# Row statistics of the first phase: joining and centring moved from VectorE to GpSimd, eight tiles at once, with longer leads

## The chip, the cores and the metric

One NeuronCore of one Trainium2 chip runs the whole program. The metric is the device time of one execution in microseconds (us). Three executions of the kernel before took 3013.57, 3014.26 and 3014.30 us.

## The reference

An adaptive-LayerNorm transformer block in fp32: x is 16 x 1024 x 256 (16 batches of 1024 rows).

```python
sa, ca, ga, sb, cb, gb = modulations of each batch            # from silu(c) @ wmod
h = layernorm(x) * (1 + ca) + sa                              # first statistics: of the rows of x
def attention(h):                                             # causal, 16 heads of 16, with rope
    hn = (h - mean(h)) * rsqrt(var(h) + 1e-5) * gamma + beta  # second statistics: of the rows of h
    q, k, v = hn @ Wq + bq, hn @ Wk + bk, hn @ Wv + bv        # rope on q and k
    return h + softmax(mask(q k^T / 4)) v @ Wo + bo
x = x + ga * attention(h)
x = x + gb * mixture_of_experts(layernorm(x) * (1 + cb) + sb) # 8 experts, 512 rows each, first two batches' rows
```

So each row of 256 values is normalised twice before the projections: once as x, once as h.

## The kernel before

The program is a chain of phases with a barrier between them: phase 0 (weights, tables, modulations), phase 1 (both normalisations, projections to q, k and v, rope, stores), phase 2 (attention), phase 3 (output projection and second residual), phase 4 (experts). The diff touches phase 1 alone, which lies between about 58 and 562 us of the span.

Phase 1 takes the 16 batches one after the other. A batch is 8 tiles of 128 rows x 256 columns (T = 8) and 4 pairs (NP = 4: q and k of each half of 512 rows). The work is laid out by hand in slots, 8 to a batch: each engine runs `slot(s)` for s from START to END in order, and each step is put into a slot by its lead: `batch_at(s, lead)` gives the batch b and the place k with s + lead = 8b + k, so a step of lead 17 comes 17 slots ahead of the slot in which projections of its batch begin. Nothing holds the engines to the same slot but semaphores; within an engine the order is fixed, and a step that waits holds up all behind it.

One batch passes through these steps (leads of the kernel before in brackets):

- SyncE `load`: x of the batch, 1 MB, into a ring of three buffers `xin`, and its modulation rows. A load waits until GpSimd has read the batch three earlier. The order in SyncE's queue is: loads 0 to 3, then for each b load b+4, the stores of b.
- VectorE `take_x` (23): `bn_stats` of two tiles in each of four slots. It gives for each row the mean of the even and of the odd columns and their sums of squared deviations (6 numbers).
- VectorE `join_x` (in take_x's last slot, L458): eight `bn_aggr`, one per tile, to mean and variance.
- ScalarE `root` (19, L554): sqrt(var + eps) of 8 tiles at once. VectorE `invert_x` (18): reciprocal (L463) and the centring term -mean/std (L465), each for 8 tiles at once.
- ScalarE `first_norm` (17, L559), one tile per slot; GpSimd `modulate` (16): times 1 + ca (L635), plus sa (L638). For batch 0 the addition is VectorE's (L473).
- VectorE `take_h` (15, L477): `bn_stats` of one tile of h per slot; `join_h` (with the last of them, L482); `root` (7); `invert_h` (6, L488, L490); ScalarE `second_norm` from lead 5 on (L566).
- TensorE transposes the tiles (L662), projects q and k (`project`, even slots, L673) and v (`values`, odd slots, L681); ScalarE copies the transposed tiles and v out of PSUM (L574, L583).
- VectorE `multiply` (odd slots, L501 and L504, four instructions of 512 columns) and `combine` (even slots, L511, L512) do the rope in PSUM. Then a split of q and k into three bf16 parts: ScalarE `high` (L591), VectorE `take_rest` (L517), ScalarE `middle` (L595), GpSimd `low` (L642, 1024 columns, even slots).
- SyncE stores v (4 DMAs), the q parts (8) and the k parts (8) of the batch.

Buffers that tie engines together: `rest` has two halves (take_rest of pair n waits for low of pair n-2), PSUM holds three pairs, `stage` and `v_st` hold two batches.

Of the kernel before, what the change touches and what calls it, by code (L numbers as in the profile page):

```python
# [17 lines left out]
F32 = mybir.dt.float32  # L18
# [3 lines left out]
ALU = mybir.AluOpType  # L22
ACT = mybir.ActivationFunctionType
# [303 lines left out]
def phase1(nc, x, ps, ident, cos_t, sin_t, w_all, bcol, rsx, nmx, mods_d, q_d, k_d, v_d):  # L327
# [11 lines left out]
    with ExitStack() as ctx:  # L339
# [5 lines left out]
        h = sb("h", [P, 2, T, D], F32)  # L345
        stx = sb("stx", [P, T, 6], F32)
        sth = sb("sth", [P, T, 6], F32)
        agx = sb("agx", [P, 2, T, 2], F32)
        agh = sb("agh", [P, 2, T, 2], F32)
        rsh = sb("rsh", [P, 2, T], F32)  # L350
        nmh = sb("nmh", [P, 2, T], F32)
        sd = sb("sd", [P, 2, T], F32)
# [8 lines left out]
        mod_in = tuple(sem(f"p1_mod_in{r}") for r in range(RING))  # L361
        stx_done, sth_done = sem("p1_stx"), sem("p1_sth")
        agx_done, agh_done = sem("p1_agx"), sem("p1_agh")
        sdx_done, sdh_done = sem("p1_sdx"), sem("p1_sdh")
        rsx_done, rsh_done = sem("p1_rsx"), sem("p1_rsh")
        ones_set = sem("p1_ones_set")
# [20 lines left out]
        def turned(n):  # L387
            return ps[:, PS_QK + n % QR * 2:PS_QK + n % QR * 2 + 2, :]

        START = -23  # L390
        END = B * T + 6

        def batch_at(s, lead):

            b, k = (s + lead) // T, (s + lead) % T
            return (b, k) if 0 <= b < B else (None, None)
# [10 lines left out]
        @block.sync  # L407
        def _(sp):
            def load(b):
                r = b % RING  # L410
                if b == RING:
                    sp.wait_ge(first_done, T)
                elif b > RING:
                    sp.wait_ge(h_done, (b - RING) * T)
                sp.dma_start(xin[:, r], x[b].rearrange("(t p) d -> p t d", p=P)).then_inc(x_in[r], DMA)
                sp.dma_start(mods[:, r], mods_d[b, 0:2, :].partition_broadcast(P)) \
                  .then_inc(mod_in[r], DMA)

            def store(b):
                p = b % 2  # L420
                sp.wait_ge(v_copied, b * T + T)
                for g in range(NG):
                    sp.dma_start(v_d[b, g], v_st[:, p, g].rearrange("p t n -> p (t n)")).then_inc(v_stored[p], DMA)
                for which, dst in enumerate((q_d, k_d)):
                    last = b * NP + NP - 2 + which
                    sp.wait_ge(hi_done, last + 1)
                    sp.wait_ge(mid_done, last + 1)
                    sp.wait_ge(lo_done, last + 1)
                    for e in range(2):
                        for g in range(NG):  # L430
                            sp.dma_start(dst[b, g, :, 32 * e:32 * e + 32, :].rearrange("s r t -> r s t"),
                                         stage[32 * g:32 * g + 32, p, :, 2 * which + e, :]).then_inc(stage_stored[p], DMA)

            for b in range(RING + 1):
                load(b)
            for b in range(B):
                if b + RING + 1 < B:
                    load(b + RING + 1)
                store(b)
            for p in range(2):  # L440
                sp.wait_ge(v_stored[p], DMA * NG * (B // 2))
                sp.wait_ge(stage_stored[p], DMA * STORES * (B // 2))

        @block.vector
        def _(dve):
# [6 lines left out]
                    ins = dve.bn_stats(stx[:, t, :], xin[:, r, t, :])  # L452
                ins.then_inc(stx_done, 1)

            def join_x(b):
                dve.wait_ge(stx_done, 4 * b + 4)
                for t in range(T):
                    ins = dve.bn_aggr(agx[:, b % 2, t, :], stx[:, t, :])  # L458
                ins.then_inc(agx_done, 1)

            def invert_x(b):
                dve.wait_ge(sdx_done, b + 1)
                dve.reciprocal(rsx[:, b, :], sd[:, 0, :]).then_inc(rsx_done, 1)  # L463
                dve.wait_ge(rsx_done, b + 1)
                dve.scalar_tensor_tensor(nmx[:, b, :], agx[:, b % 2, :, 0], -1.0, rsx[:, b, :], ALU.mult, ALU.mult) \  # L465
                   .then_inc(statx, 1)

            def take_h(b, t):
                if t == 0:
# [6 lines left out]
                    dve.wait_ge(h_done, (b - 1) * T + t + 1)  # L476
                dve.bn_stats(sth[:, t, :], h[:, b % 2, t, :]).then_inc(sth_done, 1)  # L477

            def join_h(b):
                dve.wait_ge(sth_done, b * T + T)  # L480
                for t in range(T):
                    ins = dve.bn_aggr(agh[:, b % 2, t, :], sth[:, t, :])  # L482
                ins.then_inc(agh_done, 1)

            def invert_h(b):
                p = b % 2
                dve.wait_ge(sdh_done, b + 1)
                dve.reciprocal(rsh[:, p, :], sd[:, 1, :]).then_inc(rsh_done, 1)  # L488
                dve.wait_ge(rsh_done, b + 1)
                dve.scalar_tensor_tensor(nmh[:, p, :], agh[:, p, :, 0], -1.0, rsh[:, p, :], ALU.mult, ALU.mult) \  # L490
                   .then_inc(stath, 1)

            def multiply(n):

# [24 lines left out]
            def slot(s):  # L519
                n = (s - 1) // 2  # L520
                if s % 2 == 1 and 0 <= n < B * NP:
                    multiply(n)
                n = (s - 2) // 2
                if s % 2 == 0 and 0 <= n - 1 < B * NP:
                    take_rest(n - 1)
                if s % 2 == 0 and 0 <= n < B * NP:
                    combine(n)
                b, k = batch_at(s, 18)
                if b is not None and k == 0:
                    invert_x(b)  # L530
                b, k = batch_at(s, 6)
                if b is not None and k == 0:
                    invert_h(b)
                b, k = batch_at(s, 15)
                if b is not None:
                    take_h(b, k)
                    if k == T - 1:
                        join_h(b)
                b, k = batch_at(s, 23)
                if b is not None and k < 4:  # L540
                    take_x(b, k)
                    if k == 3:
                        join_x(b)

            dve.memset(eps[:, :], EPS)
            for s in range(START, END):
# [1 line left out]

        @block.scalar
        def _(act):  # L550
            def root(b, which, ag, ready, done):
                reuse(act, rsh_done if which else rsx_done, b)
                act.wait_ge(ready, b + 1)
                nc.scalar.activation(sd[:, which, :], ag[:, b % 2, :, 1], ACT.Sqrt, bias=eps[:, :]).then_inc(done, 1)  # L554

            def first_norm(b, t):
                if t == 0:
# [37 lines left out]
                nc.scalar.copy(parts(n, 1), rest[:, n % 2]).then_inc(mid_done, 1)  # L595

            def slot(s):
                b, k = batch_at(s, 19)
                if b is not None and k == 0:
                    root(b, 0, agx, agx_done, sdx_done)  # L600
                b, k = batch_at(s, 7)
                if b is not None and k == 0:
                    root(b, 1, agh, agh_done, sdh_done)
                for tiles, b in turned_in(s - 1):
                    for t in tiles:
                        copy_x(b, t, tiles[-1])
                n = (s - 3) // 2
                if s % 2 == 1 and 0 <= n < B * NP:
                    high(n)
                if s % 2 == 0 and 2 <= s <= B * T:  # L610
                    for t in (s - 2, s - 1):
                        copy_v(t // T, t % T)
                n = (s - 5) // 2
                if s % 2 == 1 and 0 <= n < B * NP:
                    middle(n)
                b, k = batch_at(s, 17)
                if b is not None:
                    first_norm(b, k)
                for tiles, b in normed_in(s):
                    for t in tiles:  # L620
                        second_norm(b, t)
# [5 lines left out]
        @block.gpsimd  # L627
        def _(pool):
            def modulate(b, t):
                p, r = b % 2, b % RING  # L630
                if t == 0:
                    pool.wait_ge(mod_in[r], (b // RING + 1) * DMA)
                reuse(pool, xt_done, (b - 2) * T + t + 1)
                pool.wait_ge(h1_done, b * T + t + 1)
                pool.tensor_tensor(h[:, p, t, :], xin[:, r, t, :], mods[:, r, M_CA1, :], ALU.mult).then_inc(h_mul, 1)  # L635
                if b > 0:
                    pool.wait_ge(h_mul, b * T + t + 1)
                    pool.tensor_tensor(h[:, p, t, :], h[:, p, t, :], mods[:, r, M_SA, :], ALU.add).then_inc(h_done, 1)  # L638

            def low(n):  # L640
                pool.wait_ge(mid_done, n + 1)
                pool.tensor_tensor(parts(n, 2), rest[:, n % 2], parts(n, 1), ALU.subtract).then_inc(lo_done, 1)  # L642

            def slot(s):
                b, k = batch_at(s, 16)
                if b is not None:
                    modulate(b, k)
                n = (s - 6) // 2
                if s % 2 == 0 and 0 <= n < B * NP:
                    low(n)  # L650

            pool.memset(v_st[:, :, :, :, :], 1.0).then_inc(ones_set, 1)
            for s in range(START, END + 1):
                slot(s)
# [1031 lines left out]
```

## Time and profile before

| | |
|---|---|
| median of 3 runs | 3014.26 us (3013.57 to 3014.30) |
| profiled execution, its own time | 3013.66 us |
| its span | 3011.9 us |
| TensorE busy over the span | 2753.8 us, 91% |
| VectorE | 2140.9 us, 71% |
| ScalarE | 1825.3 us, 61% |
| GpSimd | 974.6 us, 32% |

The span is that of the recorded instructions; the execution's own time is 1.76 us longer. Shares of the whole span say little about one phase. In phase 1, from 100 to 500 us, VectorE is busy more than 98.7 us of each 100, TensorE 83 to 86, ScalarE 68 to 72, GpSimd 65 to 69. "Busy" is the time of an instruction; engines start the next instruction a little before the recorded end of the last, so the step from start to start is often 0.04 to 0.09 us shorter than the duration.

### The profile page before, as it was taken

The numbers are of one execution on the slowest core, as the hardware profiler recorded it, in microseconds if no ns is written. First come the engines' busy times: TensorE is split into PE (matmuls) and PEld (weight loads), VectorE is DVE, ScalarE is ACT, GpSimd is POOL, SyncE is SP. The second block draws the span as 40 slices with busy tenths as digits, with TensorE's granted clock in tenths as the row PEclk, the third lists the DMA queues.
The fourth block names the chain that finished last, engine by engine and source line by source line (L and its number), as shares of the span: only waits on it lengthen the run. The fifth ranks groups of instructions, "written<-read, shape, count | busy, mean of one in ns | idle before, by whom it ended". The sixth has DMA issues, their size and how long they took to land. (4 is left out here: it accounts for less than half of the span.)

```text
span 3011.9 us, 48208 instructions
## 1 busy us (share of the span) xinstructions
PE 2753.8 (91%) x17467; PEld 1341.3 (45%) x17467; DVE 2140.9 (71%) x3145; ACT 1825.3 (61%) x3739; POOL 974.6 (32%) x1298
## 2 busy tenths in 40 slices
PE   1788889499999999999999999999999879998997
PEld 0454445234444444444444444444444346775664
DVE  4999999587777777777777777777777436652221
ACT  1676677157777777777777777777777744441121
POOL 1666666312212212212212212212211247771331
PEclk7899999689999999999999999999999989999999
DMA  3367676824454354454454455354345068962342
GB/s 97 119 221 231 220 233 210 214 50 93 87 108 93 88 106 94 87 106 94 88 105 95 89 104 99 86 103 98 88 102 102 25 227 291 312 224 58 99 109 44
DMA packets 186485, 384.09 MB, mean 128 GB/s; under 512 B 33397, under 2 KB 102421, under 8 KB 173736
## 3 DMA queue, kind: packets, MB, share of 16 engines
q1 hardware_dynamic: 180106, 372.48, 48.2%
q0 software_dynamic: 6144, 8.52, 1.6%
q8 instruction: 141, 2.31, 0.3%
q14 instruction: 94, 0.77, 0.1%
HBM read 238.55 MB, written 144.53 MB: 127 GB/s over the span
## 5 line engine op out<-in xcount | busy, mean ns | idle before, releaser
L929 DVE TENSOR_REDUCE mx<-ps 128x2 f32<-128x1024 f32 (+3 forms) x1216 | 1371.5, 1167 | 396.9 <-PE ps L1017 301.7
L975 ACT ACTIVATE prob<-ps 128x512 f32<-128x512 f32 (+1 forms) x2560 | 1251.8, 560 | 538.8 <-PE ps L1035 530.1
L1010 PE MATMUL ps<-k_rows,q_rows 96*128 96x512 bf16 (+3 forms) x3072 | 911.2, 332 | 41.0 <-DMA k_rows<-k_parts 34.4
L1035 PE MATMUL ps<-q_rows,k_rows 99*128 99x512 bf16 (+3 forms) x3072 | 907.2, 328 | 14.7 <-ACT prob L975 6.1
L868 POOL TENSOR_SCALAR_AFFINE_SELECT prob<-prob 128x512 f32<-128x512 f32 x512 | 320.0, 637 | 1451.3 <-ACT prob L975 1451.3
L1054 PE MATMUL ps<-prob,v_rows 128*32 128x512 f32 (+3 forms) x6144 | 628.3, 496 | 0.0
L1035 PEld LDWEIGHTS ps<-q_rows,k_rows 99*128 99x128 bf16 x3072 | 273.1, 98 | 599.0 <-ACT prob L975 360.3
L1010 PEld LDWEIGHTS ps<-k_rows,q_rows 96*128 96x128 bf16 x3072 | 290.2, 98 | 271.4 <-DVE mx L929 60.5
L1017 PE MATMUL ps<-mask_b,unit_b 128*128 128x128 bf16 (+2 forms) x1408 | 348.6, 248 | 0.0
L673 PE MATMUL ps<-x_t,w_all 128*128 128x512 f32 x512 | 249.8, 634 | 0.0
L1054 PEld LDWEIGHTS ps<-prob,v_rows 128*32 128x32 f32 x6144 | 134.3, 108 | 245.8 <-ACT prob L975 122.9
L1548 DVE SCALAR_TENSOR_TENSOR y<-ps,gx,gate 128x256 f32<-128x256 f32 x32 | 15.5, 484 | 196.4 <-PE ps L1637 196.4
L1017 PEld LDWEIGHTS ps<-mask_b,unit_b 128*128 128x128 bf16 x1408 | 139.5, 99 | 22.9
L673 PEld LDWEIGHTS ps<-x_t,w_all 128*128 128x128 f32 x512 | 101.8, 207 | 105.0 <-issue 104.1
L642 POOL TENSOR_TENSOR stage<-rest,stage 128x1024 bf16<-128x1024 f32 x64 | 136.5, 2133 | 30.1 <-ACT stage L595 30.1
L1398 PE MATMUL ps<-wg,n_t 128*128 128x256 f32 x512 | 145.7, 407 | 0.0
L662 PE MATMUL ps<-ident,h 128*128 128x128 f32 x256 | 49.7, 302 | 102.3 <-ACT x_t L574 64.6
L1332 ACT COPY n_t<-ps 128x256 f32<-128x256 f32 x128 | 47.5, 371 | 148.6 <-PE ps L1386 148.3
L635 POOL TENSOR_TENSOR h<-xin,mods_b 128x256 f32<-128x256 f32 x128 | 94.0, 736 | 133.0 <-ACT xin L559 133.0
L681 PE MATMUL ps<-w_all,x_t 128*128 128x256 f32 x512 | 121.2, 379 | 0.0
L1473 POOL DMA_INDIRECT sum_rows<-ys,dest x32 | 50.4, 1574 | 212.8 <-ACT ys L1560 156.0
L1637 PE MATMUL ps<-w,hid 128*128 128x256 f32 x512 | 119.1, 386 | 0.0
(154 smaller groups left out, 2678.1 us busy)
## 6 DMA issues: line engine op xcount, KB each, us to landing
k_rows<-k_parts SPq DMA_DIRECT2D x384, 128.0 KB, 7.3
v_ones<-v_st SPq DMA_DIRECT2D x64, 512.0 KB, 4.3
v_rows<-v_ones SPq DMA_DIRECT2D x64, 512.0 KB, 9.1
att<-o_sb SPq DMA_DIRECT2D x128, 256.0 KB, 2.4
att_b<-att SPq DMA_DIRECT2D x16, 2048.0 KB, 10.1
q_parts<-stage SPq DMA_DIRECT2D x128, 192.0 KB, 3.3
k_parts<-stage SPq DMA_DIRECT2D x128, 192.0 KB, 3.3
q_rows<-q_parts SPq DMA_DIRECT2D x64, 384.0 KB, 4.6
```

Source lines behind the costliest of these rows:

```text
L642: pool.tensor_tensor(parts(n, 2), rest[:, n % 2], parts(n, 1), ALU.subtract).then_inc(lo_done, 1)
L673: ins = pe.matmul(half(n, e), w_all[:, k, c * P:(c + 1) * P], x_t[:, blk, k, :], start=(k == 0), stop=(k == KC - 1))
L681: ins = pe.matmul(o, x_t[:, t // 4, k, t % 4 * P:t % 4 * P + P], w_all[:, k, 2 * D:3 * D], start=(k == 0), stop=(k == KC - 1))
L868: pool.affine_select(out=own, in_=own, compare_op=ALU.is_ge, fill=0.0, base=0, pattern=[[0, HG], [1, P]], channel_multiplier=-1).then_inc( ...
L929: dve.tensor_reduce(dst, src, AX.X, ALU.max).then_inc(a_free, 1)
L975: nc.scalar.activation(prob[:, (g * NPC + i) % RING, h, 0:w], src, ACT.Exp).then_inc(exp_done, 1)
L1010: ins = pe.matmul(ps[:, at, col:col + w], q[0:ROWS, g, h, i * P:(i + 1) * P], k[0:ROWS, g, h, k0:k0 + w], start=(r == 0), stop=True, skip_ ...
L1017: ins = pe.matmul(own, unit_b[:, :], mask_b[:, :].rearrange("p (o n) -> p o n", o=1) .to_broadcast([P, per, P]), start=False, stop=True, s ...
L1035: ins = pe.matmul(ps[:, PS_B + bank(g, n), at:at + w], k[0:AUG, g, h, j * P:(j + 1) * P], q[0:AUG, g, h, q0:q0 + w], start=True, stop=True)
L1054: ins = pe.matmul(ps[32 * h:32 * h + 32, PS_O, col:col + w], v[:, g, j, h, :], prob[:, (g * NPC + i) % RING, h, at:at + w], start=(j == 0) ...
L1398: ins = pe.matmul(o, n_t[:, r % 2, k, :], wg[:, p, k, :], start=False, stop=(k == KC - 1))
L1637: ins = pe.matmul(o, hid[:, f, c * P:(c + 1) * P], w2[:, e % 2, f, :], start=False, stop=(f == FT - 1))
```

## The change

- The eight `bn_aggr` of a batch, for x and for h, go. GpSimd computes the same from the two half-row means and sums of squares with seven instructions over 128 x 8 values (`join`): sums, difference and spread; then the squared difference times D/4 is added to the spread; and -0.5 times the sum of means is kept as `half_sum`. Four of the seven are followed by a wait on their own semaphore (`link`). The result is 256 times the variance, and `root` scales by 1/256.
- The centring term -mean/std becomes a GpSimd product `half_sum` * reciprocal (`centre`) in a slot of its own, instead of VectorE's scalar_tensor_tensor. The reciprocals stay on VectorE.
- Leads grow: take_x 23 to 27, its join now at 23, root 22, invert 21, centre 20; first_norm 17 to 19, modulate 16 to 18, take_h 15 to 17; join of h at 9, root 8, invert 7, centre 6. second_norm and everything behind it keep theirs. START goes from -23 to -27.
- SyncE has the loads of batches 0 to 4 ahead of the first store, and load b+5 ahead of the stores of b.

```diff
-            def join_x(b):
-                dve.wait_ge(stx_done, 4 * b + 4)
-                for t in range(T):
-                    ins = dve.bn_aggr(agx[:, b % 2, t, :], stx[:, t, :])
-                ins.then_inc(agx_done, 1)
             def invert_x(b):
                 dve.wait_ge(sdx_done, b + 1)
                 dve.reciprocal(rsx[:, b, :], sd[:, 0, :]).then_inc(rsx_done, 1)
-                dve.wait_ge(rsx_done, b + 1)
-                dve.scalar_tensor_tensor(nmx[:, b, :], agx[:, b % 2, :, 0], -1.0, rsx[:, b, :], ALU.mult, ALU.mult) \
-                   .then_inc(statx, 1)
...
             def invert_h(b):
-                p = b % 2
                 dve.wait_ge(sdh_done, b + 1)
-                dve.reciprocal(rsh[:, p, :], sd[:, 1, :]).then_inc(rsh_done, 1)
-                dve.wait_ge(rsh_done, b + 1)
-                dve.scalar_tensor_tensor(nmh[:, p, :], agh[:, p, :, 0], -1.0, rsh[:, p, :], ALU.mult, ALU.mult) \
-                   .then_inc(stath, 1)
+                reuse(dve, xn_done, (b - 1) * T)
+                dve.reciprocal(rsh[:, b % 2, :], sd[:, 1, :]).then_inc(rsh_done, 1)
...
-            for b in range(RING + 1):
+            for b in range(RING + 2):
                 load(b)
             for b in range(B):
-                if b + RING + 1 < B:
-                    load(b + RING + 1)
+                if b + RING + 2 < B:
+                    load(b + RING + 2)
                 store(b)
...
+            def link(ins):
+                links[0] += 1
+                ins.then_inc(pool_chain, 1)
+                pool.wait_ge(pool_chain, links[0])
+
+            def join(b, which, st, ready, count, rooted, done):
+                pool.wait_ge(ready, count)
+                reuse(pool, rooted, b)
+                pool.tensor_tensor(sums[:, which, :], st[:, :, 1], st[:, :, 4], ALU.add)
+                pool.tensor_tensor(gap[:, which, :], st[:, :, 1], st[:, :, 4], ALU.subtract)
+                link(pool.tensor_tensor(spread[:, which, :], st[:, :, 2], st[:, :, 5], ALU.add))
+                link(pool.tensor_scalar(half_sum[:, which, :], gap[:, which, :], D / 4.0, None, ALU.mult))
+                link(pool.tensor_tensor(gap[:, which, :], gap[:, which, :], half_sum[:, which, :], ALU.mult))
+                link(pool.tensor_scalar(half_sum[:, which, :], sums[:, which, :], -0.5, None, ALU.mult))
+                pool.tensor_tensor(spread[:, which, :], spread[:, which, :], gap[:, which, :], ALU.add).then_inc(done, 1)
+
+            def centre(which, nm, rs):
+                return pool.tensor_tensor(nm, half_sum[:, which, :], rs, ALU.mult)
...
             def slot(s):                       # GpSimd
-                b, k = batch_at(s, 16)
+                b, k = batch_at(s, 23)
+                if b is not None and k == 0:
+                    join(b, 0, stx, stx_done, 4 * b + 4, sdx_done, agx_done)
+                b, k = batch_at(s, 9)
+                if b is not None and k == 0:
+                    join(b, 1, sth, sth_done, b * T + T, sdh_done, agh_done)
+                b, k = batch_at(s, 20)
+                if b is not None and k == 0:
+                    pool.wait_ge(rsx_done, b + 1)
+                    centre(0, nmx[:, b, :], rsx[:, b, :]).then_inc(statx, 1)
+                b, k = batch_at(s, 6)
+                if b is not None and k == 0:
+                    pool.wait_ge(rsh_done, b + 1)
+                    reuse(pool, xn_done, (b - 1) * T)
+                    centre(1, nmh[:, b % 2, :], rsh[:, b % 2, :]).then_inc(stath, 1)
+                b, k = batch_at(s, 18)
                 if b is not None:
                     modulate(b, k)
```

## Rows read from the trace of the kernel before

**Rows 1.** Busy time in two batch-long stretches; columns: length, then engines, clock, DMA.
```profile
141.10:170.30 29.20, 22.78 (x80) 13.47 (x80) 29.06 (x68) 20.48 (x42) 19.81 (x20) 1.00 0.72 226
287.30:316.50 29.20, 25.63 (x80) 14.77 (x80) 28.34 (x57) 20.60 (x42) 19.80 (x20) 0.88 0.69 219
```
**Rows 2.** Waits from 98 to 506 us: total us, times, longest.
```profile
POOL h L635 <- ACT xin L559: 122.5, 43, 6.0
...
DVE m L501 <- PE ps L673: 4.1, 3, 3.2
```
**Rows 3.** Instruction groups from 98.62 to 506 us: count, busy us, mean ns, idle before.
```profile
L465 DVE SCALAR_TENSOR_TENSOR nmx<-agx,rsx 128x8 f32<-128x8 f32 x13 | 21.7, 1671 | 0.4
L490 DVE SCALAR_TENSOR_TENSOR nmh<-agh,rsh 128x8 f32<-128x8 f32 x14 | 10.6, 758 | 0.5
L482 DVE BATCH_NORM_AGGREGATE agh<-sth 128x2 f32<-128x6 f32 x112 | 9.0, 153 | 0.5
L458 DVE BATCH_NORM_AGGREGATE agx<-stx 128x2 f32<-128x6 f32 x104 | 8.3, 153 | 0.4
```
**Rows 4.** VectorE in order of time: start, duration, instruction, count.
```profile
307.56 0.20 DVE L488 RECIPROCAL rsh<-sd 128x8 f32<-128x8 f32 x1
307.79 0.75 DVE L490 SCALAR_TENSOR_TENSOR nmh<-agh,rsh 128x8 f32<-128x8 f32 x1
308.46 0.41 DVE L477 BATCH_NORM_STATS2 sth<-h 128x6 f32<-128x256 f32 x1
...
315.72 0.73 DVE L452 BATCH_NORM_STATS2 stx<-xin 128x6 f32<-128x256 f32 x2
316.48 0.64 DVE L458 BATCH_NORM_AGGREGATE agx<-stx 128x2 f32<-128x6 f32 x8
317.04 1.38 DVE L501 SCALAR_TENSOR_TENSOR m<-ps,bcol,cos_t 128x512 f32<-128x512 f32 x2
```
**Rows 5.** All instructions of L465: shortest, median and longest duration.
```profile
L465 DVE SCALAR_TENSOR_TENSOR nmx<-agx,rsx x16: 166/1670/1677, 69.8 to 468.3; 128x8 f32<-128x8 f32 x16
```
**Rows 6.** GpSimd in order of time, within one batch.
```profile
322.05 2.13 POOL L642 TENSOR_TENSOR stage<-rest,stage 128x1024 bf16<-128x1024 f32 x1
324.14 0.73 POOL L635 TENSOR_TENSOR h<-xin,mods_b 128x256 f32<-128x256 f32 x1
324.95 0.73 POOL L638 TENSOR_TENSOR h<-h,mods_b 128x256 f32<-128x256 f32 x1
325.63 0.73 POOL L635 TENSOR_TENSOR h<-xin,mods_b 128x256 f32<-128x256 f32 x1
```
**Rows 7.** GpSimd's smallest instructions: two of phase 2, one at the start.
```profile
606.96 0.28 POOL L876 CAST m<-m_rest 32x128 bf16<-32x128 f32 x1 [30.27 <-DVE m_rest L912]
607.32 0.42 POOL L878 TENSOR_TENSOR m<-m_rest,m 32x128 bf16<-32x128 f32 x1
...
L1674 POOL MEMSET const-float32-0.0<- 128x1 f32 x1 | 0.1, 104 | 0.3 <-issue 0.3
```
**Rows 8.** TensorE in order of time: projection, four transposes (two tiles), values.
```profile
308.15 3.60 PE L673 MATMUL ps<-x_t,w_all 128*128 128x512 f32 x8
311.59 0.60 PE L662 MATMUL ps<-ident,h 128*128 128x128 f32 x4
312.02 1.89 PE L681 MATMUL ps<-w_all,x_t 128*128 128x256 f32 x8
```
**Rows 9.** Start of phase 1: GpSimd's first multiplications of h; VectorE's first rope instructions.
```profile
70.76 4.50 POOL L635 TENSOR_TENSOR h<-xin,mods_b 128x256 f32<-128x256 f32 x6 [5.32 <-ACT xin L559]
...
98.62 1.41 DVE L501 SCALAR_TENSOR_TENSOR m<-ps,bcol,cos_t 128x512 f32<-128x512 f32 x2 [3.21 <-PE ps L673]
```
**Rows 10.** One load of x: issue, first use; loads from 100 to 500 us, to landing.
```profile
319.79 0.69 SPq L415 DMA_DIRECT2D xin<-in_L_attn_x  x1
...
333.69 0.41 DVE L452 BATCH_NORM_STATS2 stx<-xin 128x6 f32<-128x256 f32 x1
...
xin<-in_L_attn_x SPq DMA_DIRECT2D x11, 1024.0 KB, 7.7
```

More of the change, by code:

```diff
@@ L347, in phase1 @@
         sth = sb("sth", [P, T, 6], F32)
-        agx = sb("agx", [P, 2, T, 2], F32)
-        agh = sb("agh", [P, 2, T, 2], F32)
+        sums = sb("sums", [P, 2, T], F32)
+        gap = sb("gap", [P, 2, T], F32)
+        spread = sb("spread", [P, 2, T], F32)
+        half_sum = sb("half_sum", [P, 2, T], F32)
         rsh = sb("rsh", [P, 2, T], F32)
@@ L363, in phase1 @@
         agx_done, agh_done = sem("p1_agx"), sem("p1_agh")
+        pool_chain = sem("p1_pool_chain")
         sdx_done, sdh_done = sem("p1_sdx"), sem("p1_sdh")
@@ L388, in turned @@
             return ps[:, PS_QK + n % QR * 2:PS_QK + n % QR * 2 + 2, :]
-        START = -23
+        START = -27
         END = B * T + 6
@@ L477, in take_h @@
                 dve.bn_stats(sth[:, t, :], h[:, b % 2, t, :]).then_inc(sth_done, 1)
[L479 to L483, printed above, removed]
             def invert_h(b):
-                p = b % 2
                 dve.wait_ge(sdh_done, b + 1)
-                dve.reciprocal(rsh[:, p, :], sd[:, 1, :]).then_inc(rsh_done, 1)
-                dve.wait_ge(rsh_done, b + 1)
-                dve.scalar_tensor_tensor(nmh[:, p, :], agh[:, p, :, 0], -1.0, rsh[:, p, :], ALU.mult, ALU.mult) \
-                   .then_inc(stath, 1)
+                reuse(dve, xn_done, (b - 1) * T)
+                dve.reciprocal(rsh[:, b % 2, :], sd[:, 1, :]).then_inc(rsh_done, 1)
             def multiply(n):
@@ L527, in slot @@
                     combine(n)
-                b, k = batch_at(s, 18)
+                b, k = batch_at(s, 21)
                 if b is not None and k == 0:
                     invert_x(b)
-                b, k = batch_at(s, 6)
+                b, k = batch_at(s, 7)
                 if b is not None and k == 0:
                     invert_h(b)
-                b, k = batch_at(s, 15)
+                b, k = batch_at(s, 17)
                 if b is not None:
                     take_h(b, k)
-                    if k == T - 1:
-                        join_h(b)
-                b, k = batch_at(s, 23)
+                b, k = batch_at(s, 27)
                 if b is not None and k < 4:
                     take_x(b, k)
-                    if k == 3:
-                        join_x(b)
             dve.memset(eps[:, :], EPS)
@@ L550, in _, with root @@
         def _(act):
-            def root(b, which, ag, ready, done):
+            def root(b, which, ready, done):
                 reuse(act, rsh_done if which else rsx_done, b)
                 act.wait_ge(ready, b + 1)
-                nc.scalar.activation(sd[:, which, :], ag[:, b % 2, :, 1], ACT.Sqrt, bias=eps[:, :]).then_inc(done, 1)
+                nc.scalar.activation(sd[:, which, :], spread[:, which, :], ACT.Sqrt, bias=eps[:, :], scale=1.0 / D).then_inc(done, 1)
             def first_norm(b, t):
@@ L597, in slot @@
             def slot(s):
-                b, k = batch_at(s, 19)
+                b, k = batch_at(s, 22)
                 if b is not None and k == 0:
-                    root(b, 0, agx, agx_done, sdx_done)
-                b, k = batch_at(s, 7)
+                    root(b, 0, agx_done, sdx_done)
+                b, k = batch_at(s, 8)
                 if b is not None and k == 0:
-                    root(b, 1, agh, agh_done, sdh_done)
+                    root(b, 1, agh_done, sdh_done)
                 for tiles, b in turned_in(s - 1):
@@ L615, in slot @@
                     middle(n)
-                b, k = batch_at(s, 17)
+                b, k = batch_at(s, 19)
                 if b is not None:
@@ L638, in modulate @@
                     pool.tensor_tensor(h[:, p, t, :], h[:, p, t, :], mods[:, r, M_SA, :], ALU.add).then_inc(h_done, 1)
+            links = [0]
+            def link(ins):
[14 more added lines that the diff above has]
+                return pool.tensor_tensor(nm, half_sum[:, which, :], rs, ALU.mult)
             def low(n):
```

## The prediction

> **What bounds the kernel now.** The page shows TensorE busy 91% of the span and VectorE 71%, but the diff touches only phase 1, so I read that phase alone. The busy time by batch-long windows comes first: in a batch of 29.2 us VectorE is busy 29.06, TensorE 22.78 where its clock was full, ScalarE 20.5, GpSimd 19.8 [rows 1]. The waits say the same from the other side: from the first rope instruction to 506 us VectorE waited 4.1 us in all, 3.2 of them ahead of the first, while GpSimd waited 122.5 us for ScalarE, which follows VectorE [rows 2]. So phase 1 goes at VectorE's pace, and an instruction taken from VectorE there is worth its own step. Nothing later in the program depends on when phase 1 ends except by starting then, so what phase 1 gains the program gains.
>
> **What the change removes from VectorE.** A step is start to start; the end of a recorded duration lies about 0.08 us behind the next start (0.75 from 307.79 ends at 308.54, the next starts at 308.46 [rows 4]).
> - Joins: eight bn_aggr. The statistics ahead of them start at 315.72 and would hand over after 0.73 - 0.08 = 0.65, at 316.37; the next real work starts at 317.04: 0.67, call it 0.66. After the first rope there are 104/8 = 13 joins of x and 112/8 = 14 of h [rows 3]: 8.6 + 9.2 = 17.8 us.
> - Centring term of h: reciprocal and product take 307.56 to 308.46 = 0.90 [rows 4]; the reciprocal alone, which stays, 0.20 - 0.08 = 0.12. So 0.78 each, with the mean of the product in the group near that of this one (758 ns): 14 x 0.78 = 11.0 us.
> - Centring term of x: the mean duration is 1671 ns, against 166 ns for the same instruction at its shortest [rows 3, 5]. It stretches while GpSimd works at a `low` of 2.13 us: its two inputs are both in SBUF. Its step with the gap ahead is 1.67 + 0.04 = 1.71; 13 x 1.71 = 22.2 us. Nothing on VectorE in steady state has two SBUF inputs after the change (rope and rest read one of theirs from PSUM), so that stretch does not come back elsewhere.
> Sum: 51.0 us, and VectorE's batch becomes 29.2 - 2 x 0.66 - 0.78 - 1.71 = 25.4 us.
>
> **What it adds to GpSimd.** No row shows an elementwise GpSimd instruction on 128 x 8. Bounds from the nearest: 0.10 (memset of one column) and 0.42 (subtraction of 32 x 128) [rows 7]. From L635 and L642, 0.73 at 256 columns and 2.13 at 1024 [rows 6], a straight line leaves 0.26 at none; from 0.42 at 128 and 0.73 at 256 it leaves 0.11. I take 0.20, between them. A wait for its own semaphore adds 0.08 (606.96 + 0.28 = 607.24, next at 607.32); without one the next starts 0.04 early (324.95 + 0.73 against 325.63). A join is then 2 x 0.16 + 4 x 0.28 + 0.20 = 1.64 us (bounds 1.0 and 3.2), a centring product 0.20 (0.1 to 0.42).
> GpSimd's batch now: a tile is 0.81 + 0.68 = 1.49, a `low` 2.09 [rows 6]: 8 x 1.49 + 4 x 2.09 = 20.3. New: 20.3 + 2 x 1.64 + 2 x 0.20 = 24.0 us (22.5 to 27.5), under VectorE's 25.4, but only by 1.4. Its free time was 9 us a batch; that is what hides the joins, and if each cost 2.4 it would be used up (20.3 + 4.8 + 0.4 = 25.5).
>
> **What queues behind the new waits.** In slot 1 of a batch GpSimd waits for the last statistics of x, done at the end of VectorE's slot 0. So the two are in step there once a batch. Walking GpSimd from that point (VectorE's 25.4 us spread over its slots by what each holds: 2.7 and 3.1 by turns, 3.6 and 3.3 where two tiles of x, 0.65, are added): its slots end at 3.1, 6.9, 8.4, 12.2, 13.7, 17.3, then join of h to 19.5 (it starts with VectorE's last bn_stats of h, 17.8), 21.0, 24.6. Next comes the wait to 25.4. Each tile of h is needed by VectorE late in the slot after, each `low` at the start of two slots after (slot 2's at 8.9, done 6.9): all in time. ScalarE has 20.5 us of work in 25.4 and now finds the joins a slot early; it does not stick. The reciprocal gets new waits that are a batch old: nothing.
> The Trainium skill speaks against this move: "Perfetto Trace Analysis", section "Optimizing Scalar/DVE Operations", says that work moved between VectorE and GpSimd may not help, since both share a read port. Here the row of the stretched product agrees that they block each other, but the change takes away the only VectorE instruction that was blocked; by that rule the products' 33 us would come back as GpSimd waits, and the gain would be near 15 us. Nothing above or below uses this.
>
> **TensorE** needs for a batch four projections of 3.44, four `values` of 1.73 (1.89 less the same overlap), and eight tiles at 0.215 [rows 8]: 22.4 us at full clock; in a batch of granted clock 0.88 that would be 25.4, a tie [rows 1].
>
> **Loads.** A load was issued at 319.79, needed at 333.69, and lands in 7.7: 6.2 us to spare [rows 10]. New: load c stands behind the k stores of batch c-6, whose last `low` is in slot 8c-36, with take_x in 8c-27, that is 8 slots or 25.4 us later. Less some 6 us of store issues and 7.7, 11 us to spare. The edit costs nothing. DMA share rises from 0.72 to 0.72 x 29.2/25.4 = 0.83, still not full.
>
> **The start.** Leads grow, so more precedes the first rope. First tile of h on GpSimd: was 70.76 [rows 9]; the chain before it loses 0.67 and 0.2, gains 1.64, 0.20 and a hop: 71.96. From there GpSimd runs to the second tile of batch 2, which VectorE needs in slot 0: 8 multiplications at 0.75 (4.50/6), then 10 tiles at 1.49, four joins, three products, and about 2.3 us of waits for statistics: 6.0 + 14.9 + 6.6 + 0.6 + 2.3 = 30.4, at 102.4. VectorE then has a bn_stats of h and a pair of x (0.34 + 0.65): first rope at 103.4, against 98.62: 4.8 later. In exchange VectorE has done 2 bn_stats of h and 4 pairs of x more by then: 0.7 + 2.6 = 3.3 us not to be done later.
>
> **The end.** From 506 us on nothing of the statistics is left and VectorE's work on a pair is under TensorE's 5.2 (3.44 + 1.73); the statistics of x end four slots earlier and of h two, so VectorE meets TensorE's pace sooner: I put 1.5 us on it, four such slots at some 0.4. Closing stores and barrier are unchanged. For new small waits in steady state, 2 us.
>
> **Sum** against the profiled execution: 3013.66 - 51.0 - 3.3 + 4.8 + 1.5 + 2 = 2967.7; against the median 3014.26 (0.6 above) 2968.3. I say 2968.
>
> **Rivals.**
> A. GpSimd becomes the bound. For: only 1.4 us of slack and no row of such a size. Against: the straight lines put an instruction at 0.11 to 0.26. With every price at its upper row a join is 3.2, a product 0.42, the batch 27.5: 13 x 1.7 = 22 gained, less 1.5 at the start and 4 x 1.6 more there: 14 us gained, 3000. At a join of 2.6 the batch is 26.0, the gain 13 x 3.2 - 1.5 - 4 - 2 = 34, 2980.
> B. TensorE becomes the bound, by its clock. For: granted clock 0.88 in one batch; against: that batch held a long idle of TensorE, which goes with ScalarE's sticking. At 0.85 a batch is 26.3: 0.9 x 13 = 12 us less, 2980.
> C. Slower: the chain of sixteen GpSimd instructions a batch, at y us each with waits, holds up the tiles of h. The gain is 13 x (29.2 - 20.3 - 16y), less 1.5 and 4 x (7y - 1.64) at the start; it is nil at y = 0.51. At y = 0.60 a batch is 29.9, and the time 13 x 0.7 + 1.5 + 10.2 = 21 us more, 3035. For: nothing but the upper row with its wait, 0.50. Against: the same lines.
> D. VectorE's time turns into waits in a loop over GpSimd and ScalarE, which show no more than today's pace: 3012.
>
> **Chances.** Forecast (2959 to 2975) 0.62, A 0.18, B 0.12, C 0.04, D 0.04. The low end is joins at 1.0 (start 2.6 sooner) and no small waits or tie: 2962, less 3 for the sizes of steps. The high end, 2996, takes in B and most of A. Faster by over 0.2% (6 us, about what a measurement of this kernel can tell) 0.92, within it 0.04, slower 0.04.
>
> **What would show it.** Batches of 25.4 us in phase 1, with VectorE busy about 25 of them; joins of about 1.6 us on GpSimd and GpSimd busy 23 to 24; first L501 near 103.4; phase 2 starting 46 us earlier. A VectorE that waits for GpSimd's h at every tile means A; waits at L501 for TensorE mean B. The prediction is wrong if the batch stays above 26 us.

## The result and the profile after

The changed kernel takes 2964.84 us (2964.05 to 2966.78, four runs) against 3014.28 us for the kernel before beside it: ratio 0.9835, 95% interval 0.9823 to 0.9847, that is 49 us less. The forecast was 2968, with 2959 to 2996. The profiled execution took 2965.41 us, its span is 2963.7 (before: 3013.66 and 3011.9), so the two traces differ by 48.2 us. One of the executions of the half-statistics kernel below ran at a granted clock of 0.83 and took 3243.83 us against 2947 to 2952 for the other three, and is not in its median.

First, two batch-long stretches of phase 1 in the changed kernel, to hold against [rows 1] (same columns):

```profile
core 0: us, PE busy (x) PEld busy (x) DVE busy (x) ACT busy (x) POOL busy (x), PEclk, DMA share, GB/s
260.94:286.13 25.19, 24.02 (x80) 13.38 (x80) 25.19 (x47) 20.30 (x43) 22.84 (x37) 1.00 0.85 257
286.13:311.32 25.19, 24.01 (x80) 13.40 (x80) 25.19 (x47) 20.30 (x43) 22.84 (x37) 1.00 0.88 271
```

The batch is 25.19 us, and VectorE is busy for all of it. ScalarE's work is what it was; GpSimd's busy time went from 19.8 to 22.8. TensorE is busy 24.0 us, at full clock. The waits from 103 to 460 us, the answer to [rows 2]:

```profile
ACT stage L572 <- DVE ps L497: 62.2, 41, 1.8
...
PE ps L680 <- ACT x_t L555: 9.4, 11, 0.9
...
POOL sums L632 <- DVE stx L455: 8.6, 12, 0.8
...
POOL sums L632 <- DVE sth L471: 3.7, 12, 1.6
...
DVE sth L471 <- POOL spread L638: 2.1, 1, 2.1
DVE m L486 <- PE ps L691: 1.6, 2, 1.0
```

VectorE itself stands 4.1 us in the whole window; the others wait for it, directly or through ScalarE. GpSimd, which stood 122.5 us for ScalarE, now waits where it needs VectorE's last statistics, once a batch 0.7 us for those of x and 0.3 us for those of h. In the kernel before, ScalarE stood at the head of its slot in `root` for VectorE's joins, up to 4.1 us at a time, and TensorE for ScalarE's copies of the transposed tiles, up to 4.3 us (98 to 506 us):

```profile
ACT sd L554 <- DVE agx L458: 51.4, 13, 4.1
PE ps L662 <- ACT x_t L574: 61.3, 24, 4.3
```

The second became 9.4 us with 0.9 at the longest; the first is gone from the steady batches.

VectorE's order of time around the reciprocals, for [rows 4], where joins and products are gone:

```profile
284.82 1.45 DVE L489 SCALAR_TENSOR_TENSOR ps<-ps,bcol,sin_t 128x512 f32<-128x512 f32 x2
286.13 0.23 DVE L476 RECIPROCAL rsh<-sd 128x8 f32<-128x8 f32 x1
286.24 0.42 DVE L471 BATCH_NORM_STATS2 sth<-h 128x6 f32<-128x256 f32 x1
286.54 1.25 DVE L502 TENSOR_TENSOR rest<-ps,stage 128x1024 f32<-128x1024 f32 x1
...
291.81 0.23 DVE L460 RECIPROCAL rsx<-sd 128x8 f32<-128x8 f32 x1
291.92 0.42 DVE L471 BATCH_NORM_STATS2 sth<-h 128x6 f32<-128x256 f32 x1
```

GpSimd's join of x and what follows it, the instructions for which [rows 7] gave only bounds:

```profile
283.71 0.21 POOL L632 TENSOR_TENSOR sums<-stx 128x8 f32<-128x8 f32 x1 [0.75 <-DVE stx L455]
283.88 0.21 POOL L633 TENSOR_TENSOR gap<-stx 128x8 f32<-128x8 f32 x1
284.05 0.21 POOL L634 TENSOR_TENSOR spread<-stx 128x8 f32<-128x8 f32 x1
284.34 0.23 POOL L635 TENSOR_SCALAR half_sum<-gap 128x8 f32<-128x8 f32 x1
284.66 0.20 POOL L636 TENSOR_TENSOR gap<-gap,half_sum 128x8 f32<-128x8 f32 x1
284.95 0.23 POOL L637 TENSOR_SCALAR half_sum<-sums 128x8 f32<-128x8 f32 x1
285.26 0.20 POOL L638 TENSOR_TENSOR spread<-spread,gap 128x8 f32<-128x8 f32 x1
285.42 0.72 POOL L616 TENSOR_TENSOR h<-xin,mods_b 128x256 f32<-128x256 f32 x1
286.22 0.73 POOL L619 TENSOR_TENSOR h<-h,mods_b 128x256 f32<-128x256 f32 x1
286.91 0.20 POOL L641 TENSOR_TENSOR nmh<-half_sum,rsh 128x8 f32<-128x8 f32 x1
```

An instruction takes 0.20 to 0.23 us, a step is 0.17 without a wait and 0.29 to 0.32 with one, the join 283.71 to 285.42 = 1.71 us.

Last the start, from the changed kernel's VectorE and GpSimd, for [rows 9]:

```profile
60.15 0.06 DVE L526 MEMSET eps<- 128x1 f32 x1 [2.01 <-PEq L122]
...
103.97 0.43 DVE L471 BATCH_NORM_STATS2 sth<-h 128x6 f32<-128x256 f32 x1 [2.12 <-POOL spread L638]
...
107.23 1.41 DVE L486 SCALAR_TENSOR_TENSOR m<-ps,bcol,cos_t 128x512 f32<-128x512 f32 x2 [0.69 <-PE ps L691]
```
```profile
73.79 2.27 POOL L616 TENSOR_TENSOR h<-xin,mods_b 128x256 f32<-128x256 f32 x3 [0.78 <-ACT xin L540]
78.11 0.31 POOL L632 TENSOR_TENSOR sums<-stx 128x8 f32<-128x8 f32 x1 [2.05 <-DVE stx L455]
```

The 48.2 us by part, from the two traces. Phase 1 begins for VectorE (the memset of eps) at 58.58 before and 60.15 after, 1.57 later; the same code ran ahead of it, the twelve runs below put it between 58.07 and 59.59, and a second run of the unaltered changed kernel is one of them, at 58.56, so this is no part of the change. From there to the first rope 40.04 became 47.08: 7.0 us lost. From the first rope to VectorE's first instruction of phase 2 (98.62 to 562.71, 107.23 to 515.47) 464.1 became 408.2: 55.9 us won. The rest, 2449.2 and 2448.2, is the same within 1 us.

### The profile page after: what moved, and what is told of

It is laid out like the page before. It is cut to its first block and busy times, and to the rows that moved or that the text cites. A ratio compares the mean times of both kernels' runs of the same rounds, so it can differ in the third digit from the quotient of the medians.

```text
span 2963.7 us, 48232 instructions
## 1 busy us (share of the span) xinstructions
PE 2746.7 (93%) x17467; PEld 1331.8 (45%) x17467; DVE 2086.2 (70%) x2857; ACT 1822.0 (61%) x3739; POOL 1021.1 (34%) x1554
## 5 line engine op out<-in xcount | busy, mean ns | idle before, releaser
L691 PE MATMUL ps<-x_t,w_all 128*128 128x512 f32 x512 | 232.7, 598 | 0.0
L1035 PEld LDWEIGHTS ps<-mask_b,unit_b 128*128 128x128 bf16 x1408 | 139.2, 99 | 22.8
L691 PEld LDWEIGHTS ps<-x_t,w_all 128*128 128x128 f32 x512 | 94.7, 192 | 94.1 <-issue 93.3
L1364 POOL TENSOR_TENSOR res_b<-res_b,a_b 128x256 f32<-128x256 f32 x128 | 96.2, 751 | 59.2 <-ACT res_b L1325 58.9
L1641 PE MATMUL ps<-gx_t,w 128*128 128x512 f32 x256 | 114.8, 602 | 1.3 <-ACT hid L1586 0.4
```

The costliest lines, as they stand in the source:

```text
L691: ins = pe.matmul(half(n, e), w_all[:, k, c * P:(c + 1) * P], x_t[:, blk, k, :], start=(k == 0), stop=(k == KC - 1))
L1035: ins = pe.matmul(own, unit_b[:, :], mask_b[:, :].rearrange("p (o n) -> p o n", o=1) .to_broadcast([P, per, P]), start=False, stop=True, s ...
L1641: ins = pe.matmul(ps[:, PS_H + f % 2, :], w1[:, e % 2, k, f * P:(f + 1) * P], gx_t[:, k, :], start=(k == 0), stop=(k == KC - 1))
```

## The experiments

A batch is measured below from one reciprocal of h to the next; "start" is from the memset of eps to the first rope. Before 29.2 (29.1 to 29.9) and 40.0; changed 25.2 and 47.1. In the cuts of code below `...` marks what is left out, and a line that lists leads sums up the edits to them.

**The leads alone.** The kernel before with the new leads, START and loads.

```diff
-        START = -23
+        START = -27
-            for b in range(RING + 1):      # and load(b + RING + 1) in the loop
+            for b in range(RING + 2):      # and load(b + RING + 2)
...
-   take_x 23, root 19/7, invert 18/6, first_norm 17, modulate 16, take_h 15
+   take_x 27, root 22/8, invert 21/7, first_norm 19, modulate 18, take_h 17
```

> The kernel before with the new leads, START and loads, joins and products still on VectorE. If the gain is VectorE's removed work (main theory): a batch stays at 29.2 us, the first rope comes some 3 us later and is mostly paid back, 3012 to 3018 us. If the gain came from the looser leads (rival): a batch well under 29, 3000 us or less.

Measured 3004.98 us (ratio 0.9967, 0.9953 to 0.9981): a batch of 28.82, a start of 40.2. Neither theory gave this size: 9 us less than the 3014 of the kernel before. The start is not late at all, so the 7 us of the changed kernel are not the leads'. And the batch fell by 0.4, while the two products became 0.55 shorter in sum: the slots decide what GpSimd is doing when a product comes up. VectorE's two products in this kernel, from the first rope on:

```profile
L491 DVE SCALAR_TENSOR_TENSOR nmh<-agh,rsh 128x8 f32<-128x8 f32 x15 | 24.0, 1603 | 0.5
...
L465 DVE SCALAR_TENSOR_TENSOR nmx<-agx,rsx 128x8 f32<-128x8 f32 x13 | 3.6, 275 | 0.4
```

Against [rows 3] the two have changed places: x fell from 1671 to 275 ns, h rose from 758 to 1603. One of each engine from the same trace shows what they wait for:

```profile
301.26 1.86 DVE L491 SCALAR_TENSOR_TENSOR nmh<-agh,rsh 128x8 f32<-128x8 f32 x1
```
```profile
300.97 2.13 POOL L643 TENSOR_TENSOR stage<-rest,stage 128x1024 bf16<-128x1024 f32 x1
```

The product ends at 303.12, GpSimd's subtraction at 303.10. It is so in the kernel before too: there the product of x ends at 324.20, the `low` of [rows 6] at 324.18.

```profile
322.53 1.67 DVE L465 SCALAR_TENSOR_TENSOR nmx<-agx,rsx 128x8 f32<-128x8 f32 x1
```

The leads did one thing more. TensorE's long waits for ScalarE's copies are gone in this kernel already (108 to 455 us), and its granted clock reads 1.00 in each of three stretches of 100 us, where the batches of the kernel before read 0.88 to 1.00:

```profile
PE ps L663 <- ACT x_t L575: 14.4, 23, 1.0
```

**Products back on VectorE**, joins on GpSimd, all else as changed.

```diff
                 dve.reciprocal(rsx[:, b, :], sd[:, 0, :]).then_inc(rsx_done, 1)
+                dve.wait_ge(rsx_done, b + 1)
+                dve.tensor_tensor(nmx[:, b, :], half_sum[:, 0, :], rsx[:, b, :], ALU.mult).then_inc(statx, 1)
...                                          # the same for h; GpSimd's centre steps go, its join waits for statx / stath
```

> The changed kernel with only the two centring products put back on VectorE (tensor_tensor, both inputs in SBUF), joins left on GpSimd. Main theory: each product waits out the GpSimd instruction in progress, 0.1 to 2.1 us each, 0.7 on the mean with GpSimd 90% busy: a batch of 26.6 us instead of 25.2, 2984 us (2968 to 3010), the duration of the two products spread between 0.17 and 2.2 us. Rival, that the stretch went with the old slots and not with the two SBUF inputs: products at 0.17 us, 2967.

Measured 2977.55 us (0.9874, 0.9857 to 0.989), batch 26.2. The mean was over-sized, the mechanism right: the products take 274 and 583 ns on the mean (shortest 166, longest 1245), not the 0.17 of the rival. Products and their gaps are 1.0 us of the batch. The product of h now comes up beside a multiplication by GpSimd of 0.7 us and not beside a `low` of 2.1, and ends with it, at 292.19 and 292.16:

```profile
291.61 0.58 DVE L480 TENSOR_TENSOR nmh<-half_sum,rsh 128x8 f32<-128x8 f32 x1
```
```profile
291.44 0.72 POOL L623 TENSOR_TENSOR h<-h,mods_b 128x256 f32<-128x256 f32 x1
```

**Joins back on VectorE**, products on GpSimd (as a negation and a product). In the cut `ag`, `st`, `nm` and `rs` stand for those of x and of h.

```diff
+                ins = dve.bn_aggr(ag[:, b % 2, t, :], st[:, t, :])     # join_x, join_h as before, new leads
...
+                pool.tensor_scalar(negm, ag[:, b % 2, :, 0], -1.0, None, ALU.mult)
+                pool.tensor_tensor(nm, negm, rs, ALU.mult)
```

> New leads, bn_aggr joins back on VectorE, the centring products on GpSimd (a negation and a product each). Main theory: 1.3 us a batch more than the changed kernel's 25.2, 26.5, times 13 = 17 us more, less some 5 us at the start where GpSimd no longer holds up the tiles of h: 2975 to 2980. If the joins were hidden before and brought nothing: 2960 to 2967.

Measured 2975.25 us (0.9868, 0.9852 to 0.9885), as expected. The batch is 26.51, 1.32 over the changed kernel's: the two joins at 0.66 of the prediction. The start is 40.8, so it is the joins on GpSimd that make it late.

**Joins twice.** The seven instructions run once more into scratch, ahead of the real ones, with a wait on the last as well.

```diff
                 reuse(pool, rooted, b)
+                pool.tensor_tensor(sums2[:, which, :], st[:, :, 1], st[:, :, 4], ALU.add)
...                                          # the other six, with their links
```

> The changed kernel with every join's seven instructions done twice on GpSimd (the first set into scratch), 1.8 us more a join. GpSimd's batch goes from 24.0 to 27.6 us. If GpSimd was 1 us from being the bound: batches of 27.6 us, 13 x 2.4 = 31 us, and at the start five joins, 9 us: near 3003. If GpSimd has slack enough that VectorE still sets the pace: 2966 to 2975.

Measured 3007.25 us (0.9977, 0.9966 to 0.9987): batch 27.7 (27.7 to 27.8), start 55.4. GpSimd is the bound here and nearly eats the gain. Its stretch and VectorE's waits (from 108 to 455 us):

```profile
281.91:309.71 27.80, 25.01 (x80) 14.41 (x80) 25.59 (x48) 20.51 (x42) 25.61 (x51) 0.94 0.73 223
```
```profile
ACT sd L536 <- POOL spread L646: 58.8, 26, 4.2
...
DVE sth L472 <- POOL spread L646: 19.0, 13, 3.9
DVE sth L472 <- POOL h L620: 6.0, 14, 1.2
```

VectorE is busy 25.6 us, near the 25.2 of the changed kernel, in 27.8; most of the missing two are waits for the join (`sth` has one buffer, so the first bn_stats of a batch waits for the join of the last) and for tiles of h: 19.0 + 6.0 us in 12.5 batches, 2.0 a batch.

**Three more instructions a join**, without waits, 1.0 us a batch.

```diff
+                pool.tensor_tensor(sums2[:, which, :], st[:, :, 1], st[:, :, 4], ALU.add)
+                pool.tensor_tensor(gap2[:, which, :], st[:, :, 1], st[:, :, 4], ALU.subtract)
+                pool.tensor_tensor(spread2[:, which, :], st[:, :, 2], st[:, :, 5], ALU.add)
```

> The changed kernel with three more instructions of 128 x 8 in each join, without waits, 0.17 us each: GpSimd's batch goes from 24.05 to 25.05 us, still under VectorE's 25.2. If GpSimd costs nothing until it is the bound: 2.5 us more from the five joins of the start and none after, 2967 to 2968. If the cost is in proportion to GpSimd's work (a threshold already passed): 13 us more for the batches as well, 2980.

> The changed kernel itself, unaltered, as a measure beside the next two on the same chip: 2965 (2963 to 2967).

Measured 2968.15 us (0.9849, 0.9836 to 0.9863), and the unaltered changed kernel beside it 2963.88 (0.9834, 0.9821 to 0.9847). The batch is 25.2 as it was; the start is 48.7 against 46.5. Of the 4.3 us between the two medians the start explains 2.2 and the steady batches nothing; the rest is not assigned, and each interval is 4 us to either side. So GpSimd's work costs nothing in the batch up to about 25 us, and in full beyond it: joins twice, 27.6 us of work, gave 27.7.

**Half the statistics.** Both bn_stats read 128 of the 256 columns, so the kernel normalises by the statistics of half a row.

```diff
-                    ins = dve.bn_stats(stx[:, t, :], xin[:, r, t, :])
+                    ins = dve.bn_stats(stx[:, t, :], xin[:, r, t, 0:D // 2])
...                                          # the same for h
```

> The changed kernel with both bn_stats over 128 of the 256 columns (the statistics are of half a row), some 2 us a batch off VectorE. If GpSimd at 24.0 us of its own work is the next bound: batches of 24 to 24.2 us, 13 x 1.1 = 14 us less, 2950, VectorE waiting for GpSimd's h. If only TensorE at 22.4 stands behind VectorE: batches of 23.1, 2937.

Measured 2948.8 us (2947.4 to 2952.4; ratio 0.9784, 0.9764 to 0.9803). One batch:

```profile
297.17:321.22 24.05, 23.27 (x81) 13.52 (x80) 23.27 (x47) 20.51 (x42) 22.74 (x37) 1.00 0.89 279
```
```profile
315.09 0.29 DVE L471 BATCH_NORM_STATS2 sth<-h 128x6 f32<-128x128 f32 x1 [0.58 <-POOL spread L638]
```

The batch stops at 24.05, which is GpSimd's own work by steps: 8 x 1.49 + 4 x 2.09 + 2 x 1.70 + 2 x 0.16 = 24.0. GpSimd is the next bound, 1.1 us behind VectorE; TensorE, busy 23.3 us, is not yet one.

**Old leads under the new work.** GpSimd joins and products, but leads, START and loads of before.

```diff
-        START = -27
+        START = -23
...
-   take_x 27, join 23/9, root 22/8, invert 21/7, centre 20/6, first_norm 19, modulate 18, take_h 17
+   take_x 23, join 19/7, root 19/7, invert 18/6, centre 17/6, first_norm 17, modulate 16, take_h 15
```

> The changed kernel's GpSimd joins and products under the leads, START and loads of the kernel before (join of x in take_x's next slot, product one slot ahead of first_norm, join of h just ahead of its root). Main theory: VectorE still sets the pace, since a GpSimd that is late by some 1 us waits less for the reciprocal: 25.2 us a batch, and an earlier first rope, 2958 to 2968. Rival, that the looser leads are needed once GpSimd is in the chain: VectorE waits in each batch for the join or the root, 1 us or more: 2980 or over.

Measured 3024.20 us (1.003, 1.0017 to 1.0043): slower than the kernel before. My theory fell here. VectorE is as relieved as in the changed kernel, 25.4 us of work, but its batch is 29.4 on the mean (28.8 to 30.5). One of the shorter:

```profile
284.77:313.66 28.89, 24.10 (x81) 14.23 (x80) 25.39 (x47) 20.51 (x44) 22.85 (x36) 0.94 0.73 227
```

The waits of this kernel from 108 to 430 us:

```profile
ACT sd L535 <- POOL spread L638: 87.5, 22, 4.5
...
PE ps L680 <- ACT x_t L555: 54.2, 22, 3.9
...
DVE m L486 <- PE ps L691: 20.2, 13, 3.4
DVE rest L502 <- ACT stage L572: 18.0, 15, 1.9
```

Read from below it is a chain: VectorE waits for TensorE's projections and ScalarE's copies, TensorE for the copies of transposed tiles, ScalarE stands at the head of its slot in `root`, four us at a time, for a join. The join itself takes 1.7, but it comes in GpSimd's queue behind a `low` of 2.1: in one batch the `low` starts at 305.78, the join at 307.89, `root` at 309.74 after 3.79 us of waiting. It is the loop of the prediction's rival D. The kernel before stood in `root` in the same way, for VectorE's joins, but there VectorE had work of its own for the whole batch.

**Root last.** The same kernel, with ScalarE's two roots moved from the head of its slot to the end.

```diff
             def slot(s):                       # ScalarE
-                ... root(b, 0, agx_done, sdx_done) ... root(b, 1, agh_done, sdh_done)
                 ...                            # copies, high, middle, norms
+                ... root(b, 0, agx_done, sdx_done) ... root(b, 1, agh_done, sdh_done)
```

> The kernel of the old leads with GpSimd joins (3024 us, 28.9 us a batch), with ScalarE's root moved from the head of its slot to the end. Theory from that run's trace: ScalarE stands in root for the join, 4 us twice a batch, and so holds up its copies of the transposed tiles, which holds TensorE and then VectorE. Then the batch falls to 26 to 27 us, 2980 to 2995. Rival, that the reciprocals' own wait on the late root holds VectorE: still 28 us or more, 3010 or over.

Measured 2979.37 us (0.9882, 0.9866 to 0.9897), batch 26.7: 45 us of the 59 come back by moving the two waits behind the work that others need. So the chain over ScalarE is shown. Of the 1.5 us a batch still missing, VectorE's waits from 108 to 430 us, 12 batches, name 1.2: 7.5 us for joins, 3.7 for the loads in their old place, 2.7 for projections.

**Old loads** under the changed kernel.

```diff
-            for b in range(RING + 2):      # and load(b + RING + 2) in the loop
+            for b in range(RING + 1):      # and load(b + RING + 1)
```

> The changed kernel with the loads in SyncE's old place (b+4 ahead of the stores of b). By slots: load c stands behind the k stores of batch c-5, whose last low is in slot 8c-28, one slot before take_x needs it; stores 5.9 us and landing 7.7 us then fall on VectorE, 13 us in each of 12 batches: 3070 to 3130, VectorE waiting for the DMA of xin. If the loads had slack anyway: 2965.

Measured 3095.01 us (1.0264, 1.0247 to 1.0282), batch 37.2 (36.6 to 37.9). One wait of VectorE and the issue of a load:

```profile
342.17 0.75 DVE L455 BATCH_NORM_STATS2 stx<-xin 128x6 f32<-128x256 f32 x2 [12.06 <-DMA xin<-in_L_attn_x]
```
```profile
328.92 5.81 SPq L434 DMA_DIRECT2D k_parts<-stage  x8
334.78 0.45 SPq L418 DMA_DIRECT2D xin<-in_L_attn_x  x1
```

The load leaves behind eight stores, at 334.78, and VectorE goes on at 342.17, 7.4 later. The new leads can't be had without the new place of the loads: 130 us. What that place would be worth under the old leads was not run.

**The start on VectorE.** The changed kernel, with bn_aggr and scalar_tensor_tensor on VectorE for the first four batches of x and the first two of h.

```diff
+                    if k == 3 and b < EARLY_X:          # EARLY_X, EARLY_H = 4, 2
+                        join_early(b, stx, agx, stx_done, 4 * b + 4, agx_done)
...
-                if b is not None and k == 0:
+                if b is not None and k == 0 and b >= EARLY_X:
                     join(b, 0, stx, stx_done, 4 * b + 4, sdx_done, agx_done)
```

> The changed kernel, but the joins and products of the first four batches of x and the first two of h, which fall before the first rope, are bn_aggr and scalar_tensor_tensor on VectorE. If the start is late because GpSimd's queue holds the joins (main theory): first rope 40 us after the phase's begin as with the leads alone, not 47, steady batches the same 25.2: 2958 (2955 to 2961). If the leads themselves make the start late: 2965.

> The kernel with the early joins and products on VectorE once more, against the changed kernel on one chip: 4 to 7 us less than it, 2959 to 2961, since the first rope comes 6.7 us sooner after the phase's begin.

Measured 2960.87 us (0.9817, 0.98 to 0.9833), and again, beside the changed kernel's 2963.88, 2958.72 (0.9822, 0.9808 to 0.9835): 5.2 us less than the changed kernel, with no execution of the one among those of the other (2958.03 to 2962.38, and 2963.26 to 2967.08), and the fastest here of those that normalise by whole rows. Start 40.5 and 40.6, batch 25.2. In the changed kernel's start of 47.1 us GpSimd is busy 36.8 and VectorE 23.1, with waits for tiles of h and for joins; here they are busy 30.3 and 27.3 of 40.5. So early in the phase the work belongs on the other engine than later.

## Why the prediction was right, point by point

- **VectorE sets the pace, and what it sheds is gained in full.** Shown: 25.19 us a batch against the 25.4 forecast, 100% busy. Step by step the batch is 29.2 before, 28.8 with the new leads and loads, 26.5 with the products on GpSimd too, 25.2 with the joins as well.
- **Joins 0.66 each.** Shown (26.51 against 25.19 with both back), for a kernel whose products are already on GpSimd. In the other order the joins are worth more, 28.8 to 26.2, in part since their move also shortened the products (1.88 to 0.86 us a batch, next point).
- **Products, 33 us.** The reason held: they wait out GpSimd's instruction. The size holds for the old leads and loads only; under the new ones the products were worth 2.3 us a batch with the joins on VectorE (28.8 to 26.5), 30 us in thirteen, and 1.0 with the joins on GpSimd. The 0.4 that the leads took off the batch, 5 us in thirteen, more than makes up the difference. But the price isn't the product's own. It is set by what GpSimd has in hand when the slot comes: 2.43 us a batch under the old leads, 1.88 under the new, 0.86 once the joins had shifted GpSimd (means of the two products added; the last pair are tensor_tensor, the others scalar_tensor_tensor). The Trainium skill, "Perfetto Trace Analysis", section "Optimizing Scalar/DVE Operations", says that moving work between these two engines might not help, since they share a read port. The traces agree that the one waits for the other (301.26 + 1.86 against 300.97 + 2.13), but the advice was not borne out: with no instruction of two SBUF inputs left on VectorE in the steady batches, what the products had cost did not come back as waits of GpSimd, which stood 12.3 us in all for VectorE's statistics from 103 to 460 us.
- **GpSimd's instruction 0.20, join 1.64, batch 24.0.** Measured 0.20 to 0.23, 1.70, 24.0. The slack of a little over 1 us is real on both sides: 1.0 more costs nothing, 3.6 more sets the pace. Rival A was the right rival, and its turning point was where the sum had it.
- **TensorE** kept its full clock; rival B did not occur. It was busy 24.0 us of the 25.2 where the prediction had summed 22.4, so by busy time its room was 1.2 us and not 3; in the half-statistics kernel that time shrank to 23.3, so part of it is not work of its own. The prediction laid its long idle to ScalarE's sticking; that both went with the leads alone (61.3 us of waits for copies, then 14.4) bears this out, and it is then the leads that removed rival B, not the joins.
- **The start, 4.8 predicted, 7.0 measured.** Mis-sized terms: the first tile 0.3, GpSimd's queue 1.2 (waits 2.9 for 2.3, joins 1.70 to 1.81 for 1.64), TensorE's projection 0.7 late on top (its eight matmuls took 6.00 us at a granted clock of 0.60, against 4.89 at 0.74 before). In a second run of the changed kernel the matmuls took 5.41 us and the start was 46.5. The prediction puts the lateness down to the leads first; the runs put it on the joins (start 40.2 with the leads alone, 40.8 with the joins back, 40.5 with the early joins and products back).
- **The reserves.** 2 us for small waits and 1.5 for the tie at the end were not needed, and the batch was 0.2 shorter than forecast, 2.6 us over thirteen. From the first rope on, 50.8 us were forecast (51.0 + 3.3 - 3.5) and 55.9 came: with the start's 2.2 the other way the total is right to 3 us partly by luck, two errors that cancel.
- **What I did not see:** the leads. I costed them at a loss at the start and nothing else. Without them the same relief of VectorE brings no gain at all (3024 us): ScalarE stands in `root` for GpSimd's join, and the copies that TensorE needs stand behind it. Rival D, to which the prediction gave 0.04, is what happens there. My walk of the slots took the new leads as given and so came out right; asked about the old ones I was wrong by some 60 us. The loads I had counted as costless in the same way; they are what makes the leads possible.

## What to carry to other kernels

In this kernel moving work off the bounding engine was worth its steps only once the new hop had a slot of its own: put one slot between producer, root, reciprocal and product, or else put the waiting instruction behind the work that others need. Where the instruction in question waits for another engine, as the products here, its price changes with every other move, so measure the moves in both orders. Count the receiving engine's batch by steps from start to start, and expect no cost in the steady state until it meets the pace, and the full cost after. Where an engine is the bound in the steady state, it may be idle at the start: split the work by phase, not by kind.

## What was not expected of the hardware

- VectorE's product of two SBUF operands, 128 x 8, took from 0.166 to 1.87 us. From the first rope on every one longer than 0.17 us ended 0.01 to 0.04 us after the GpSimd instruction then running, in the kernel before, with the leads alone and with the products back. The same instruction cost 1671 ns on the mean in the kernel before and 275 where only the leads and the loads were new.
- GpSimd does arithmetic on 128 x 8 fp32 at a step of 0.17 us without a wait (inputs with a stride of six) and 0.29 to 0.32 with one on its own semaphore: waits among such small instructions cost nearly as much as the instructions (0.12 to 0.15 each).
- TensorE's granted clock in steady batches, 0.88 to 1.00 before, was 1.00 in every batch-long stretch read of the changed kernel, in which no wait of TensorE was over 0.9 us. Before, a wait of 4.27 us ahead of 288.29 was followed by a projection of 6.14 us at a granted clock of 0.57 instead of 3.60; after waits of 2.58 and 2.04 us in the batch from 141.10 the projections took 3.60. Under the old leads with GpSimd joins waits of 3.74 and 3.75 us were followed by projections of 4.50 (clock 0.79) and 5.29 (0.67), and the batch's clock was 0.94.
